# A two-layer decoder on one core: keys and values four sequences ahead, loads in need order, a table of priorities, and PSUM operands for VectorE

## The reference

```
x = x + L0_attn(layernorm(x))          # 16 heads of 8, causal, softmax
x = x + L0_xattn(layernorm(x), ctx)    # 8 heads of 64, keys and values from ctx, bias
x = x + L0_ffn(layernorm(x))           # ternary weight, input rounded to integers in [-128, 127]
x = x + L1_attn(layernorm(x))          # 16 heads of 8, scores clipped to +-10, causal, softmax
x = x + L1_xattn(layernorm(x), ctx)    # 16 heads of 64, keys and values from ctx
x = x + L1_ffn(layernorm(x))           # 8 experts, softmax gate, gates under 0.1 dropped and the rest normalised
```

## Time and profile before

| | |
|---|---|
| median of 3 runs | 623.97 us (621.42 to 626.67) |
| profiled execution, device time | 621.14 us |
| its span | 619.3 us |
| TensorE matmul busy | 536.3 us, 87% of the span |
| ScalarE, VectorE, GpSimd busy | 439.0, 426.4 and 408.5 us (71, 69 and 66%) |
| mean granted TensorE clock | 0.977 |

### The profile page before, as it was taken

One profiled execution on the slowest core, in us unless ns is written; L12 is line 12 of the kernel. 1 busy time (PEld: TensorE's weight loads), 2 busy tenths in 40 slices (PEclk: granted clock), 3 DMA queues, 4 the chain that ended last, 5 costly groups with the idle time before them and its releaser, 6 DMA issues.

```text
span 619.3 us, 15587 instructions
## 1 busy us (share of the span) xinstructions
PE 536.3 (87%) x5299; PEld 420.4 (68%) x5314; DVE 426.4 (69%) x888; ACT 439.0 (71%) x1169; POOL 408.5 (66%) x566
## 2 busy tenths in 40 slices
PE   1877788898898989898999999899999998989983
PEld 0554557776676777686777777687877776768651
DVE  0555758768689767877787886877777867574542
ACT  1545676896786778688786778787887887857650
POOL 3445567679486874867776878768775767575533
PEclk9998989999899999999999999999999999979997
DMA  8300000000000000000000000000000000000000
GB/s 274 147 1 2 1 1 2 3 1 2 2 2 7 2 6 1 2 7 1 6 2 5 4 5 1 6 3 6 2 1 7 2 6 2 6 6 1 6 5 10
DMA packets 5838, 8.55 MB, mean 14 GB/s; under 512 B 896, under 2 KB 4352, under 8 KB 5760
## 3 DMA queue, kind: packets, MB, share of 16 engines
q1 hardware_dynamic: 5760, 7.55, 3.6%
HBM read 6.50 MB, written 1.05 MB: 12 GB/s over the span
## 4 chain that ended last, share of the span: by engine, by line
PE 43%; issue 15%; POOL 15%; POOLq 10%; ACT 8%; DVE 7%; DVEq 1%; ACTq 0%
PE X L918 7%; PE S L968 7%; POOL w_low_self L546 6%; POOL diff_cross L553 5%; PE S L956 4%; PE X L1003 4%; PE S L943 4%; PE X L994 4%; PE X L1047 3%; PE S L1082 3%; POOLq L520 3%; ACT e_cross L623 2%; PE S L929 2%; POOLq L563 2%; POOLq L537 2%
## 5 line engine op out<-in xcount | busy, mean ns | idle before, releaser
L546 POOL TENSOR_TENSOR w_low_self<-w_self 128x1024 f16<-128x1024 f32 x64 | 129.9, 2040 | 49.3 <-ACT w_self L614 40.4
L623 ACT ACTIVATE e_cross<-S,row_max_cross 128x128 f32<-128x128 f32 x384 | 103.7, 419 | 6.0 <-DVE row_max_cross L740 6.0
L553 POOL TENSOR_TENSOR diff_cross<-e_cross,e_rec_cross 128x1024 f32<-128x1024 f32 x48 | 91.9, 1918 | 15.9 <-DVE e_rec_cross L749 15.6
L740 DVE TENSOR_REDUCE row_max_cross<-S 128x8 f32<-128x1024 f32 x48 | 57.3, 1218 | 35.9 <-PE S L956 35.8
L747 DVE TENSOR_REDUCE e_sum_cross<-e_cross 128x8 f32<-128x1024 f32 x48 | 58.4, 1216 | 17.2 <-ACT e_cross L623 17.1
L968 PE MATMUL S<-ident,diff_cross 128*128 128x128 f32 x384 | 52.3, 281 | 12.7 <-ACT e_cross L623 6.0
L632 ACT ACTIVATE w_cross<-S 128x1024 f32<-128x1024 f32 x48 | 50.7, 1056 | 11.5 <-PE S L968 9.4
L968 PEld LDWEIGHTS S<-ident,diff_cross 128*128 128x128 f32 x384 | 44.0, 145 | 16.7 <-ACT e_cross L623 7.1
L956 PE MATMUL S<-kT_cross,qT_cross 64*128 64x128 f32 x768 | 53.3, 286 | 2.1 <-ACT w_self L614 1.3
L994 PE MATMUL X<-w_cross,v_cross 128*64 128x128 f32 x768 | 51.2, 280 | 4.2 <-ACT v_cross L590 2.6
L956 PEld LDWEIGHTS S<-kT_cross,qT_cross 64*128 64x128 f32 x768 | 46.9, 192 | 11.2 <-issue 7.9
(11 more groups left out here) (159 smaller groups left out, 1350.5 us busy)
## 6 DMA issues: line engine op xcount, KB each, us to landing
out_dram<-x_moe SPq DMA_DIRECT2D x16, 64.0 KB, 1.5
x_all<-in_x SPq DMA_DIRECT2D x1, 960.0 KB, 7.2
cT_all<-in_ctx SPq DMA_DIRECT2D x1, 960.0 KB, 9.2
e_k<-in_e_k SPq DMA_DIRECT2D x1, 512.0 KB, 7.6
e_v<-in_e_v SPq DMA_DIRECT2D x1, 512.0 KB, 8.2
e_q<-in_e_q SPq DMA_DIRECT2D x1, 512.0 KB, 9.0
e_o<-in_e_o SPq DMA_DIRECT2D x1, 512.0 KB, 10.4
m_w<-in_m_w SPq DMA_DIRECT2D x1, 512.0 KB, 8.9
```

Of the source, the lines that this page charges most:

```text
L546: pool.tensor_tensor(L.w_low[u][:], L.w[u][:], halves(L.w[u][:]), ALU.subtract)\
L553: pool.tensor_tensor(L.diff[u][:].rearrange("p (h k) -> p h k", h=UNIT), L.e[u][:].rearrange("p (h k) -> p h k", h=UNIT), L.e_rec[:, u, :] ...
L623: last = act.activation(L.e[u][:, P * p:P * (p + 1)], S_[:, P * p:P * (p + 1)], ACT.Exp, bias=L.row_max[:, u, p:p + 1])
L740: dve.tensor_reduce(L.row_max[:, u, :], group(i, turn)[:].rearrange("p (h k) -> p h k", h=UNIT), AX_X, ALU.max, negate=True).then_inc(L.ma ...
```

## The change

- `kT` and `v` of the two cross attentions exist four times (`AHEAD`), so keys and values may be made up to four sequences ahead of their use. `e` and `diff` of a cross attention become one tile, written by the exp and divided in place.
- The loads are issued in another order and cut in more groups: sequence 0 of `x`, `a_qk`, `a_v`; sequences 1 to 3 of `x`; sequences 0 to 3 of `ctx`, `b_k`, `b_v`; the rest of the first layer; `e_k`, `e_v`; and only then the remaining 12 sequences of `x` and of `ctx` and the other weights. ScalarE runs one exp on a 128 x 1 tile at its start.
- `Plan` adds an entry of a table `FORWARD` (in ns, one for nearly every step) to the priority, `LAG` is 9700, and several costs are edited.
- VectorE operations that read and wrote SBUF are moved: the bounds of `self1` are put on the raw scores in PSUM, ahead of the exp (`bd` before `ex`, the exp then in place in SBUF); the rounding of `ffn` comes after the transpose, in PSUM, and takes over what ScalarE's `xTe` did there (that transpose is now of f32); the reciprocals of a self attention's sums, the exponentials of the gate and the kept gates lie in unused columns of a PSUM bank. The gate's bank is thus held from `g` until the gates are done, where it was given back after the first addition.

```diff
+AHEAD = dict(cross0=4, cross1=4)
+EARLY = 4
...
         if L == "ffn":
             add(f"{L}.qz", "DVE", 1000, [f"{L}.nm"], [f"{L}.res"])
-            add(f"{L}.un", "ACT", 400, [f"{L}.qz"], [f"{L}.rd"])
-            add(f"{L}.rd", "DVE", 650, [f"{L}.un"], [f"{L}.xT"])
-        fill(f"{L}.xT", xT, [f"{L}.rd" if L == "ffn" else f"{L}.nm"], f"{L}.xTe", users)
-        add(f"{L}.xTe", "ACT", 185, [f"{L}.xT"])
+            add(f"{L}.un", "ACT", 330, [f"{L}.qz"], [f"{L}.xT"])
+        fill(f"{L}.xT", xT, [f"{L}.un" if L == "ffn" else f"{L}.nm"], f"{L}.xTe", users)
+        add(f"{L}.xTe", *(("DVE", 520) if L == "ffn" else ("ACT", 185)), [f"{L}.xT"])
...
-                add(f"{L}.ex.{u}", "ACT", 1020, [f"{L}.s2"])
-                add(f"{L}.bd.{u}", "DVE", 1250, [f"{L}.ex.{u}"])
-                add(f"{L}.lo.{u}", "POOL", 1900, [f"{L}.bd.{u}"])
+                add(f"{L}.bd.{u}", "DVE", 1150, [f"{L}.s2"])
+                add(f"{L}.ex.{u}", "ACT", 1050, [f"{L}.bd.{u}"])
+                add(f"{L}.lo.{u}", "POOL", 1900, [f"{L}.ex.{u}"])
...
-            fill(f"{L}.k.{c}", 900, [loads], f"{L}.ke.{c}", [f"{L}.s1.{c}"])
+            fill(f"{L}.k.{c}", 900, loads, f"{L}.ke.{c}", [(f"{L}.s1.{c}", AHEAD[L])])
...
-            fill(f"{L}.v.{c}", 870, [loads], f"{L}.ve.{c}", [f"{L}.pv.{c}"])
+            fill(f"{L}.v.{c}", 870, loads, f"{L}.ve.{c}", [(f"{L}.pv.{c}", AHEAD[L])])
...
-    fill("moe.g", 150, ["moe.xTe", "in.moe"], "moe.lg", ["moe.w"])
+    fill("moe.g", 150, ["moe.xTe", "in.moe"], "moe.w")
...
-LAG = 9500
+LAG = 9700
+
+FORWARD = {
+    "self0.st": -5200, "self0.rs": 2500, "self0.nm": -2100, "self0.xT": 18100, "self0.xTe": -7300,
...
-                name = max(ready, key=lambda n: tail[n] - LAG * at[n])
+                name = ready[0] if engine == "SP" else max(ready, key=lambda n: tail[n] + FORWARD.get(n, 0) - LAG * at[n])
...
-        LOADS = dict(first=["a_qk", "a_v", "a_o"], cross0=["b_k", "b_v", "b_q", "b_o", "b_bias", "f_w"],
-                     x=[], ctx=[], self1=["d_qk", "d_v", "d_o"], cross1=["e_k", "e_v", "e_q", "e_o"],
-                     moe=["m_g", "m_gb", "m_w", "m_b"])
+        LOADS = dict(x0=[], first=["a_qk", "a_v"], x1=[], c0=["b_k", "b_v"],
+                     more=["a_o", "b_q", "b_o", "b_bias", "f_w"], kv1=["e_k", "e_v"], x=[], ctx=[],
+                     self1=["d_qk", "d_v", "d_o"], cross1=["e_q", "e_o"], moe=["m_g", "m_gb", "m_w", "m_b"])
+        SLICES = dict(x0=(x_all, "x", 0, 1), x1=(x_all, "x", 1, EARLY), x=(x_all, "x", EARLY, NSEQ),
+                      c0=(cT_all, "ctx", 0, EARLY), ctx=(cT_all, "ctx", EARLY, NSEQ))
...
                 if L is self1:
-                    act.wait_ge(s_full, score(i, "self1.s2"))
-                    act.activation(L.w[u][:], group(i, "self1.s2", u)[:], ACT.Exp, scale=SD ** -0.5, bias=shift[:])\
-                        .then_inc(taken(i, "self1.s2", u)[0], 1)
+                    act.wait_ge(*taken(i, "self1.s2", u))
+                    act.activation(L.w[u][:], L.w[u][:], ACT.Exp, scale=SD ** -0.5, bias=shift[:])\
+                        .then_inc(L.weighed[u], 1)
...
             act.wait_ge(consts, N_CONSTS)
+            act.activation(table[:], eps[:], ACT.Exp)
...
             def round_units(i):
-                dve.wait_ge(units_ready, i + 1)
-                dve.tensor_scalar(a_clip[:], a_unit[:], Q_MAX, -Q_MAX - 1, ALU.min, ALU.max)
-                dve.drain()
-                if i:
-                    dve.wait_ge(x_full, full(i - 1, "ffn.xT"))
-                dve.tensor_scalar(a_int[:], a_clip[:], ROUND, -ROUND, ALU.add, ALU.add).then_inc(rounded, 1)
+                units = bank(i, "ffn.xT")[:, 0:P]
+                dve.wait_ge(x_full, full(i, "ffn.xT"))
+                dve.tensor_scalar(units, units, Q_MAX, -Q_MAX - 1, ALU.min, ALU.max)
+                if i:
+                    dve.wait_ge(x_full, full(i - 1, "ffn.y"))
+                dve.drain()
+                dve.tensor_scalar(a_intT[:], units, ROUND, -ROUND, ALU.add, ALU.add)\
+                    .then_inc(emptied(i, "ffn.xT")[0], 1)
...
             def bound(L, i, u):
-                w = L.w[u][:].rearrange("p (h q) -> p h q", h=UNIT)
-                dve.wait_ge(*taken(i, f"{L.name}.s2", u))
-                dve.scalar_tensor_tensor(out=w, in0=w, scalar=W_LOW,
-                                         in1=w_bound[:].unsqueeze(1).broadcast_to([P, UNIT, P]),
-                                         op0=ALU.max, op1=ALU.min).then_inc(L.bounded[u], 1)
+                name = f"{L.name}.s2"
+                dve.wait_ge(s_full, score(i, name))
+                if i:
+                    dve.wait_ge(x_full, full(i - 1, f"{L.name}.pv"))
+                dve.scalar_tensor_tensor(out=L.w[u][:].rearrange("p (h q) -> p h q", h=UNIT),
+                                         in0=group(i, name, u)[:].rearrange("p (h q) -> p h q", h=UNIT),
+                                         scalar=-CLIP * SD ** 0.5,
+                                         in1=s_bound[:].unsqueeze(1).broadcast_to([P, UNIT, P]),
+                                         op0=ALU.max, op1=ALU.min).then_inc(taken(i, name, u)[0], 1)
...
                 dve.drain()
-                dve.reciprocal(L.o_rec[:], L.o_sum[:, :, SD])
+                dve.reciprocal(o_rec, L.o_sum[:, :, SD])
...
-                dve.tensor_scalar(g_soft[:], g_exp[:], g_rec[:], None, ALU.mult)
-                dve.drain()
-                dve.scalar_tensor_tensor(out=g_kept[:], in0=g_soft[:], scalar=THRESHOLD, in1=g_soft[:],
+                dve.tensor_scalar(g_soft[:], gates(i, 1), g_rec[:], None, ALU.mult)
+                dve.drain()
+                dve.scalar_tensor_tensor(out=gates(i, 2), in0=g_soft[:], scalar=THRESHOLD, in1=g_soft[:],
```

193 lines of the change are left out of this document (97 added, 96 removed), and 19 rows, old and new, of the table FORWARD.

## The result

The changed kernel takes 572.79 us (median of 4 runs, 570.44 to 573.36), the kernel before 625.02 in the same job (621.42 to 626.67): a ratio of 0.9164, interval 0.9115 to 0.9214, 8.4% faster. The four executions have spans of 568.6 to 571.6 us at granted clocks of 0.985 to 0.975; the profiled one (571.0) is among the longer.

A forecast was written before the change was run, and what follows sets the result against it. TensorE was taken as the bound. Idle -16.8 (start), -12 (middle), +2 (end) and work +1 - 2 made -28 us: 593 us from the profiled execution, 596 us against the median, range 579 to 613.

The forecast's parts named there:

- What bounds the kernel: Whole span: TensorE is the bound, its matmuls filling 536.3 of 619.3 us, with 83.0 us idle.
- The start, 16.8 us: First 100 us: loads, early table load and lead cut TensorE's idle from 32.5 to 15.7 us; bounds 8 and 22.
- The lead gives no second gain in the middle: Middle: the lead is spent once, and from sequence 7 on the order has it at one sequence again.
- The middle, 12 us: Middle: table and operands bring idle to the settled half's 5.5%, 24 us against 36.0; bounds nothing and 27.
- The operands, nothing beside the 12: VectorE and GpSimd: most of 8.5 and 9.4 us of waits should go, but neither is the bound, so nothing added.
- `g_weight` near its 232 ns, `w_low` near 1893: Gates and GpSimd, a sign: means near these medians, from 764 and 2040 ns; if high, operands didn't part the engines.
- The end, 2 us of idle, and 32 us long: From cross1's last scores: chain stays about 32 us, idle grows by 2 us as values move ahead; bounds 0 and 5.
- TensorE's work, -1: TensorE's busy time: f32 transposes of ffn add about 1 us, a better granted clock takes 2 off; clock bounds 0 to 5.
- ScalarE's exp of `self1` from SBUF: ScalarE: 32 exps reading SBUF cost 0.11 us more each, 3.5 us; 1.4 by the skill; nothing counted.
- Rival 2: The middle closes: filler and free GpSimd and VectorE leave TensorE 2% idle there; -43 us, 581 us; chance 0.15.
- Rival 3: The gate holds an `X` bank too long, TensorE stands until one is emptied: slower, 631 us; chance 0.06.
- Rival 1: Only the start pays: the middle keeps 36 us, a new order trading one wait for another; 608 us; chance 0.22.

The follow-up runs named there:

- pairs without a table: Kernel before with new loads, and that plus a four-sequence lead: 615.78 and 600.69 us; the same two with PSUM operands added: 606.61 and 606.37 us.
- fitted pair: Changed kernel with a lead of one sequence against the changed kernel with its full lead, each with a newly fitted priority table: 579.12 and 562.55 us.
- fit_before: Operands, lead and loads of the kernel before, with early table load, cross1's weights in two steps, one e/diff tile and a fitted priority table: 602.32 us.
- small_in_sbuf: Changed kernel, same lists and banks, with gates, self-attention reciprocals and the first of two rounding steps back in SBUF: 581.46 us.
- psum_loads: Kernel before plus the new loads, early table load and VectorE's PSUM operands, without lead or table: 606.61 us, ratio 0.9735.
- warm_tail: Changed kernel plus 27 extra bfloat16 matmuls on TensorE in the last sequence, results overwritten: 569.07 us, ratio 0.9145.
- parted_gate: Changed kernel plus one VectorE instruction writing the soft gates again into PSUM, where the thresholding reads one operand: 568.71 us, ratio 0.9133.
- late_loads: Changed kernel with the other engines' lists identical and only SP's loads in about the sequence of before: 574.15 us, ratio 0.9239.
- lag_9500: Changed kernel with the planner's LAG at 9500 in place of 9700, whole priority table kept: 616.7 us.
- runs with a misfit table: Changed kernel with PSUM operands, lead or loads undone one at a time, its priority table kept: 654.55, 619.47 and 620.34 us.

## Why the prediction was wrong

- **What bounds the kernel.** Right: TensorE bound it and still does; the span's gain of 48.3 us is 44.5 of idle time and 3.8 of work.
- **The start, 16.8 us.** Measured 18.6, and its steps as told: first row maximum at 14.22 (about 15), `e_k` there at 21.86. The runs confirm what pays: the lead, 7 us of the start in the pairs without a table (25.6 to 18.3, 25.5 to 18.6), 11.2 in the fitted pair that differs in nothing else. The loads matter less than the prediction's story of them: with `x` and the keys' weights of `cross1` late at the same order the start loses 2.7 us, and `fit_before`, with the old loads, idles 24.5 us there where before idled 32.5.
- **The lead gives no second gain in the middle.** Right: 5.4 and 5.0 us of idle, without and with it.
- **The middle, 12 us. This is the step that failed.** Measured 26.2. I took the settled half's 5.5% for the whole middle, "as the nearest row that this kernel has reached", and let table and operands share it. `fit_before` shows what the order gives alone: with the operands of before, 24.7 us of idle in 469.7, 5.3%, and a gain of 12.4. So 12 us are what an order gives alone; the other 14 of the 26.2 were reached only with the operands on PSUM (10.9 us of idle and less, against 22.0 and more). For this kernel the row was no limit; that it nearly agrees with `fit_before` may be chance, since one table there is one sample.
- **The operands, nothing beside the 12.** The second half of the same error. I had priced the waits themselves, 8.5 us of VectorE and 9.4 of GpSimd, and then wrote that neither engine is the bound, so that they count nothing. `small_in_sbuf` puts three of them at 8.7 us at a fixed order, the fitted pairs put all of them at 17 to 19 us of the middle, and `psum_loads`, with no table and no lead, at 10.8 us of it. In a kernel whose TensorE waits a microsecond here and there on every engine, a microsecond on an engine that is 69% busy is on TensorE's path each time its result is the next thing needed.
- **`g_weight` near its 232 ns, `w_low` near 1893.** Both right, 226 and 1895, and yet "the operands part the two engines" is only half true: the wait of the gates moved to L843. The prediction looked at the instruction that had waited and not at another one of the chain that could.
- **The end, 2 us of idle, and 32 us long.** Idle grew by 0.2 only, but last scores to end are 36.3 us for 34.2 before, and to the last `x_moe` 34.3 for 32.2: longer by the 2 us, filled with work at a granted clock of 0.79 instead of 0.89 (the last four expert matmuls take 3.76 us, before 3.34). The sum put the 2 us down as idle behind the values that had moved; the busy time says otherwise. `warm_tail` shows that the clock is worth 3 us there.
- **TensorE's work, -1.** Measured -3.8, inside its bounds, but within what one kernel varies: `parted_gate` and `late_loads`, with the same matmuls, are busy 527.7 and 529.0 us against 532.5.
- **ScalarE's exp of `self1` from SBUF.** I took 0.11 us more each. It is 1145 ns (L628) against 1114 from PSUM in the kernel before: 31 ns. The Trainium skill, VectorE: DVE Perf Modes, section "The TRN2 errata — SBUF-src ops pay a fixed extra latency per instruction", has 52 cycles between the two sources, an estimate of 43 ns, nearer than the row I took. By the same table the prediction estimated the two roundings on PSUM as 131 ns longer each, 4.2 us in all. They are 290 and 292 ns there; in the kernel before they took 227 each when they did not wait (a median and a least), so a PSUM operand costs about 64 ns, half the estimate. With the waits their means were 414 and 441. (The 4.2 us would also be a quarter of the 17.9 that the waits cost, not a third.)
- **Rivals.** Rival 2 had half of the mechanism, and 0.15: free GpSimd and VectorE close the middle, its filler doesn't (5.4 us of idle without the lead, 5.0 with it). It asked for 2% idle in the middle, which came out at 2.5%. Start, work and end came out 1.8, 2.8 and 1.8 us better than in its sum, the middle 0.8 worse; that is 5 of the 8 us by which it missed, and the 2.8 us that were added to come from one execution to the median are the rest. Rival 3's bank is not in the waits: what TensorE waits for of the gates is their result `g_weight` (1.9 us). Rival 1, a new order that trades one wait for another, is what `lag_9500` and the runs with a misfit table did.

## What to carry to other kernels

A row of a kernel's best stretch is a limit only for what that stretch already has: before it is taken as the end of a term, each change that removes something from it (here the operands) has to be priced on its own. In a kernel with fixed lists a priority table belongs to one configuration; to learn what another part is worth, give each variant an order that fits it, or keep the lists word for word and change the operands under them, but don't undo a part and keep the table. And where one instruction's wait is taken away, look at the next one with the same kind of operands: the wait may just move on.

## What the runs showed of the hardware

- **VectorE behind GpSimd.** What waits is not only an instruction with two SBUF inputs. `a_intT <- a_clip` has one, with both sides in SBUF, and takes 226 to 1830 ns; with its input in PSUM 291 to 293. `g_soft` from SBUF has a mean of 963, from PSUM 226. A reciprocal of 8 columns in SBUF stays at 202. The Trainium skill, SBUF — State Buffer, section "SBUF: two separate sides", has the rule: VectorE operations in a two-port mode or with two SBUF inputs and GpSimd's lock each other out for a whole instruction. The trace agrees: the waits go up to one GpSimd operation of 1.90 us, and the waiting one ends with it (188.76 and 188.74).
- **The clock at the end.** After 3.56 us of idle the four expert matmuls took 3.76 us at a granted clock of 0.50, 1.2 GHz; behind 3.62 us of matmuls in bfloat16 that do nothing 1.96 us at 1.00, 2.4 GHz. The windows of these stretches, the changed kernel's first:

```profile
560.20:563.90 3.70, 3.70 (x6) 1.35 (x6) 1.50 (x9) 0.39 (x2) 0.00 (x0) 0.50 0.00 0
```
```profile
557.90:559.80 1.90, 1.90 (x6) 0.67 (x5) 0.95 (x6) 0.39 (x2) 0.00 (x0) 1.00 0.00 0
```

So in this pair the clock that the stretch gets goes by what TensorE did ahead of it, and the idle time before a chain's last large step can be filled for it.
